# Mixer decays from running sums, an attention stage written out on TensorE, and the output bias as a one-row product

## The chip, the core and the metric

The kernel runs on one core of one Trainium2 chip. The metric is the device time of a whole execution in microseconds. The time of the kernel before is the median of three runs; one further execution was taken by the profiler, and all rows shown come from it. TensorE is written PE in the rows, VectorE DVE, ScalarE ACT, GpSimd POOL, the sync engine with its DMA queue SP.

## What is computed

A decoder layer over 32 sequences of 128 tokens with 128 features, each of its three parts followed by a layer norm. The mixer is a recurrence over tokens with four heads:

```python
alpha = jnp.exp(A_t * dt_t); beta = (1 - tr_t) * dt_t * alpha; gamma = tr_t * dt_t
base = bt * (px * beta + xt * gamma)
sr = sr * alpha + concatenate([base[..., :R] * cos(th), base[..., R:]])
si = si * alpha + base[..., :R] * sin(th)
y = sum((sr[..., :R] * cos(th) + si * sin(th)) * ct[..., :R]) + sum(sr[..., R:] * ct[..., R:])
...
x1 = layernorm(x + (y + D * x_h) * silu(z_h) @ w_out.T)
x2 = layernorm(x1 + softmax(mask(q k^T / sqrt(8))) v @ Wo + bo)
out = layernorm(x2 + shared_expert(x2) + routed_experts(x2))
```

For a pair of tokens s <= t of a sequence the factor of the recurrence is exp(sum of A*dt over the tokens after s up to t), 0 for s > t. Attention is over 16 heads of 8 features, keys and values from a context, with a mask over the keys. The bias `bo` is an input like the others. The experts are 16 with 4 chosen, out of the best 2 of 4 groups.

## The kernel before

The sequences go in groups of four (GS = 4, 512 tokens), eight groups. Three stages follow one another, each a block at whose end all engines meet: mixer, attention, experts. Each engine has its own program, written by hand; what orders the work is the position in each program and the semaphores (`sem.at(g, k)` is the k-th event of group g). `pairs` and `ahead` run the groups: `pairs` has six groups in a loop of two and the last two written out, `ahead` has four in a loop of two and the last four written out, so in attention each engine has one jump back, after group 1.

**Setup** (a block of its own) computes the small projections, dt, A and the gates on VectorE and ScalarE for two halves of the sequences, and with GpSimd the coefficients (`coefficients`, `betas`): A*dt as `decay` and in two parts `dec_hl`, `gamma` and `beta`.

**Mixer.** For each sequence b of a group, TensorE's `front(g, par, b)` (L856 to L862) makes the sums for all pairs of tokens: two products of the triangle `after` with `ramp` (L859; A*dt spread over columns by the triangle `upto`, made by GpSimd in `ramps`, L732, two operations of 512 columns a sequence), and one that adds -30000 above the diagonal (L860, bfloat16), into the bank PD. ScalarE takes the exponential of the bank in one operation of 512 columns (L693), VectorE multiplies the scores with it (`mix`, L806). `tokens` (L868) are the projections of the present and the shifted tokens, three products of 256 columns each, the first three in `front`, the others at the head of `scores`. VectorE weighs them with gamma and beta (L791, L792) and adds them (`w_tok`, L795); `back` (L900) is the product with `mix`. `scores` also has three products of `plain` (L877) and four instructions of c_rot with b_rot (L880).

A group's order on TensorE is: `theta` of the next group (L405), `skip` (L893), then for b = 1, 2, 3: `front(b)`, `back(b-1)`, `scores(b)`, and after the first two of them `features` 0, 1 and 2, 3 of the next group (L420), then features 4, 5, `front` of the next group's first sequence, `back(3)`, first scores of the next group, `mixer_output` (L285). Features 2 and 3 write the banks from which VectorE reads b_rot and c_rot, and wait for these (`freed`). The angles of a group go theta (TensorE), `angles` (ScalarE), `fractions` (VectorE, L387 and L391, two of each), `sines` (ScalarE, L368, behind an ACT_TABLE_LOAD), `rotate` (VectorE: two b_rot at L766, four c_rot at L769 and L770). VectorE's order is mix(0), fractions, inputs and mix(1), rotate, inputs and mix(2), plain_lo, inputs and mix(3), then y (L829), gates, inputs of the next group, the residual (L124) with its statistics, and the split of x (L395) that stands at the head of the next group. GpSimd's order is ramps of this group's sequences 2 and 3, ramps of the next group's 0 and 1, `steps_of`, then `normalise_pool`. In the last group it makes the third parts of k and q (`part_third`, L237) instead, and SP's queue stores and stacks these (L265, L266, L276).

**Attention.** Scores are made twice, once for the row maxima (VectorE, L1237) and once transposed for the exponential (ScalarE, L1145); masks enter by products (L1383), the scores proper are L1393. `weigh` has the products with v (L1437) and with ones (L1433). The maxima are split in three bfloat16 parts by four short VectorE operations (`split_maxima`, L1255 to L1261, tile `npart`), transposed (L1457), stored and read back by DMA (`max_scratch`, `q_stack`). `output(g)` (L1464) multiplies the normed context with `w_o`, 128 columns of float32 for each of four sequences. GpSimd's `biased` (L1081, tile `xb`) adds `b_o` to x1 ahead of it, and VectorE's residual sum (L124) reads xb and the bank. SP stages x1 by DMA for TensorE's transposes (`xs`, L1029 and `x1T`).

**Experts** isn't touched. The line by which the features wait for what frees their banks:

```python
freed = [(s_ang, 0), (s_ang, 1), (s_prod, 1), (s_prod, 3), (s_prod, 4), (s_prod, 5)]
```

Of the kernel before, what the change touches and what calls it, by code (L numbers as in the profile page):

```python
# [23 lines left out]
P = 128  # L24
NSEQ = 32
# [264 lines left out]
def mixer(nc, t, d, psum, a):  # L290

    with ExitStack() as ctx:
# [15 lines left out]
        after = sb("after", [P, P], F32R)  # L308
        acausal = sb("acausal", [P, P], BF16)
# [5 lines left out]
        gamma = sb("gamma", [P, NSEQ, HEADS])  # L315
        beta = sb("beta", [P, NSEQ, HEADS])
        decay = sb("decay", [P, NSEQ, HEADS])
        alpha = sb("alpha", [P, NSEQ, HEADS])
        dec_hl = sb("dec_hl", [P, 2, NSEQ, HEADS])
        dec_r = sb("dec_r", [P, NSEQ, HEADS], F32R)  # L320
# [6 lines left out]

        xhl = sb("xhl", [P, 2, 2, GS, P + 1], F32R)
# [5 lines left out]
        s_coef, s_alpha = (ctx.enter_context(nc.semaphore(n)) for n in ("coefficients_pool", "alpha_ready"))  # L334
# [5 lines left out]
        s_ramp = sem("ramp_ready", 8)  # L340
        s_dec = sem("decay_mm", GS)
        s_xx = sem("x_mm", GS)
        s_g = sem("g_mm", GS)
        s_exp = sem("expo_ready", GS)
        s_w = sem("w_ready", 3 * GS)
# [8 lines left out]
        P0, P1, PX, PD, PG, PY0, PY1, PO = psum  # L354
# [28 lines left out]
        def fractions(dve, g):  # L383

            for k in range(2):
                dve.wait_ge(s_ang.sem, s_ang.at(g, k))
                dve.tensor_scalar(whole[:, k, :], ang[:, k, :], ROUND, -ROUND, ALU.add, ALU.add).then_inc(s_whole.sem, 1)  # L387
            for k in range(2):
                dve.wait_ge(s_whole.sem, s_whole.at(g, k))
                dve.wait_ge(s_trig.sem, s_trig.at(g - 1, k))  # L390
                dve.tensor_tensor(frac[:, k, :], ang[:, k, :], whole[:, k, :], ALU.subtract).then_inc(s_frac.sem, 1)  # L391
# [30 lines left out]

        def coefficients(pool, half):

            seqs, n = HALVES[half], 7 * half
            dt, dec, hi, lo = soft[:, seqs, 0:4], decay[:, seqs, :], dec_hl[:, 0, seqs, :], dec_hl[:, 1, seqs, :]
            pool.tensor_tensor(dec, dec, dt, ALU.mult).then_inc(s_coef, 1)
            pool.wait_ge(s_coef, n + 1)
            pool.tensor_copy(dec_r[:, seqs, :], dec).then_inc(s_coef, 1)
            pool.tensor_tensor(gamma[:, seqs, :], gate[:, seqs, :], dt, ALU.mult).then_inc(s_coef, 1)  # L430
# [17 lines left out]
        with ExitStack() as c1:  # L448
# [40 lines left out]
            def _(pool):  # L489
                for s in (s_ramp, s_turns):  # L490
                    s.prime(pool)
# [232 lines left out]
        def _(pool):  # L724
# [1293 lines left out]
```

## Time and profile before

| what | us |
|---|---|
| median of three runs | 678.86 (673.94 to 679.98) |
| the profiled execution | 679.41 |
| its span, first to last instruction | 677.7 |
| TensorE busy in the span | 600.6 (89%), mean granted clock 0.96 of 2.4 GHz |
| VectorE, ScalarE, GpSimd busy | 498.2 (74%), 255.8 (38%), 261.2 (39%) |
| setup until the first `theta` of the groups | 0 to 45.9 |
| mixer until the last group's `skip` | 45.9 to 222.3 |
| the last group and the passage to attention | 222.3 to 251.1 |
| attention, its head and its groups | 251.1 to 473.4 |
| experts | 473.4 to 677.7 |

A row of the timeline gives the start, the time until the last of its merged instructions ends, the engine, the line of kernel.py, the operation, out<-in, the count, and in brackets how long the engine was idle before it and what ended that. Products are pipelined: a row's time is longer than the distance to the next start, and it is the distances that add up. A float32 product of the rows counts as two instructions. "issue" is idle time for which the profile shows no event waited for.

### The profile page before, as it was taken

How to read it: one execution, taken by the hardware profiler on the slowest of the kernel's cores; microseconds unless marked ns; L12 is line 12 of the kernel's file. 1: busy time of each engine (PE TensorE's matmuls, PEld its weight loads, DVE VectorE, ACT ScalarE, POOL GpSimd, SP SyncE). 2: the span in 40 equal slices, each digit the busy share in tenths (PEclk: the TensorE clock that was granted, in tenths of full speed). 3: DMA queues.
4: the chain of work that ended last, by engine and by line, in shares of the span. 5: the costliest groups of instructions: out<-in, count | busy, mean ns of one | idle time of the engine just before them, and what ended most of it. 6: DMA issues, size and time to landing. Idle time of an engine off the chain costs nothing. (4 is left out here: it accounts for less than half of the span.)

```text
span 677.7 us, 17999 instructions
## 1 busy us (share of the span) xinstructions
PE 600.6 (89%) x6368; PEld 494.8 (73%) x6368; DVE 498.2 (74%) x1246; ACT 255.8 (38%) x444; POOL 261.2 (39%) x301
## 2 busy tenths in 40 slices
PE   6589999999999855699799999877999999999994
PEld 6467777777787643578678777655888888888884
DVE  3867977977977738368688888656688787887863
ACT  2443533533543320356446655343332232232220
POOL 4264646647645628624244346091110110110111
PEclk9979999999999978699899999899999999999998
DMA  7020000000000067064464555400000000000000
GB/s 211 0 63 1 17 15 0 15 15 0 15 16 1 12 176 219 17 171 138 124 176 117 142 133 154 119 7 2 32 1 32 31 0 32 31 29 2 17 16 16
DMA packets 39186, 39.29 MB, mean 58 GB/s; under 512 B 4609, under 2 KB 30753, under 8 KB 39121
## 3 DMA queue, kind: packets, MB, share of 16 engines
q1 hardware_dynamic: 37200, 35.69, 18.4%
q0 software_dynamic: 704, 1.92, 1.1%
q10 hardware_dynamic: 1216, 0.79, 0.5%
q8 instruction: 44, 0.72, 0.5%
q14 instruction: 22, 0.17, 0.1%
HBM read 24.10 MB, written 10.88 MB: 52 GB/s over the span
## 5 line engine op out<-in xcount | busy, mean ns | idle before, releaser
L1911 PE MATMUL bank<-xT_hl_c,w_up 128*128 128x512 f32 x432 | 119.7, 413 | 2.4 <-ACTq L67 2.4
L141 POOL TENSOR_TENSOR rstd<-mv,norm_c 128x4 f32<-128x4 f32 x24 | 6.4, 268 | 272.0 <-DVE mv L135 257.1
L1237 DVE TENSOR_REDUCE nmax<-bank 128x4 f32<-128x512 f32 x112 | 72.0, 685 | 31.0 <-PE bank L1393 26.7
L1145 ACT ACTIVATE prob<-bank 128x512 f32<-128x512 f32 x128 | 69.4, 594 | 56.1 <-PE bank L1393 46.8
L1911 PEld LDWEIGHTS bank<-xT_hl_c,w_up 128*128 128x128 f32 x432 | 77.2, 192 | 16.2 <-ACTq L67 2.6
L1833 ACT ACTIVATE sg<-bank 128x512 f32<-128x512 f32 x72 | 43.0, 597 | 106.7 <-PE bank L1911 106.7
L1927 PEld LDWEIGHTS bank<-w_down,hid 128*128 128x128 f32 x576 | 74.4, 191 | 5.9 <-issue 0.5
L732 POOL TENSOR_TENSOR ramp<-upto,dec_hl 128x512 fp32r<-128x512 f32 x64 | 66.8, 1072 | 27.2 <-PE bank L860 27.2
L1927 PE MATMUL bank<-w_down,hid 128*128 128x128 f32 x576 | 75.6, 275 | 0.0
L1383 PE MATMUL bank<-neg_i,mask 64*128 64x256 bf16 x512 | 52.7, 286 | 17.9 <-ACT prob L1145 5.8
L1866 DVE TENSOR_TENSOR gu<-sg,bank 128x512 f32<-128x512 f32 x64 | 43.9, 685 | 21.9 <-PE bank L1911 10.0
L1870 DVE TENSOR_TENSOR hid<-gu,bank 128x512 f32<-128x512 f32 x64 | 44.0, 688 | 7.1 <-DVE gu L1866 1.0
L868 PE MATMUL bank<-w_x,xhl 128*128 128x256 f32 x192 | 42.2, 329 | 0.0
L1383 PEld LDWEIGHTS bank<-neg_i,mask 64*128 64x128 bf16 x512 | 16.9, 97 | 33.2 <-issue 11.7
L1437 PE MATMUL bank<-prob,v_d 128*32 128x128 f32 x1024 | 36.4, 286 | 0.0
L1433 PE MATMUL bank<-prob,ones_s 128*32 128x128 f32 x1024 | 34.6, 276 | 0.8 <-ACT prob L1145 0.8
L420 PE MATMUL bank<-xhl,w_feat 128*128 128x512 f32 (+1 forms) x96 | 29.9, 447 | 5.4 <-DVE b_rot L766 4.4
L868 PEld LDWEIGHTS bank<-w_x,xhl 128*128 128x128 f32 x192 | 29.6, 191 | 6.1 <-issue 5.3
L880 PE MATMUL bank<-c_rot,b_rot 128*128 128x256 f32 x128 | 32.8, 378 | 0.0
L1433 PEld LDWEIGHTS bank<-prob,ones_s 128*32 128x32 f32 x1024 | 26.0, 109 | 6.1 <-issue 2.2
L1437 PEld LDWEIGHTS bank<-prob,v_d 128*32 128x32 f32 x1024 | 28.2, 114 | 2.9 <-ACT prob L1145 0.2
L1071 POOL CAST mask<-mask 128x512 bf16<-128x512 uint8 x32 | 19.3, 612 | 27.3 <-PE bank L1393 22.2
(227 smaller groups left out, 1250.1 us busy)
## 6 DMA issues: line engine op xcount, KB each, us to landing
k_stack<-k_scratch SPq DMA_DIRECT2D x32, 128.0 KB, 2.7
q_stack<-q_scratch SPq DMA_DIRECT2D x32, 128.0 KB, 2.9
k_scratch<-k_part SPq DMA_DIRECT2D x16, 192.0 KB, 2.5
q_scratch<-q_part SPq DMA_DIRECT2D x16, 192.0 KB, 2.5
x<-xT_in SPq DMA_DIRECT2D x8, 256.0 KB, 8.4
mask<-mask_in SPq DMA_DIRECT2D x8, 256.0 KB, 4.7
xres<-x_in SPq DMA_DIRECT2D x8, 256.0 KB, 2.9
k_stack<-k_scratch SPq DMA_DIRECT2D x32, 64.0 KB, 3.0
```

Source lines behind the costliest of these rows:

```text
L732: pool.tensor_tensor(ramp[:, b % 2, v, :, :], bc(upto[:, None, :], [P, HEADS, P]), bc(dec_hl[:, v, bass.ds(g * GS + b, 1), :].rearrange("p ...
L868: mm = pe.matmul(PX[:, shift * D_INNER:(shift + 1) * D_INNER], xhl[:, par, a, b, 1 - shift:P + 1 - shift], w_x[:, v, :], start=(n == 0), s ...
L1145: act.activation(prob[:, b % 2, ORDER[n], :, :], (TT0, TT1)[n % 2][:, :], ACT.Exp, scale=XD ** -0.5)\
L1237: dve.tensor_reduce(nmax[:, b, 4 * u:4 * u + 4], (SS0, SS1)[n % 2][:, :].rearrange("p (i k) -> p i k", i=4), AX_X, ALU.max, negate=True).t ...
L1383: pe.matmul(banks[j][:, :].rearrange("p (i h k) -> p i h k", i=4, h=2)[:, :, half, :], mask[rows, par, b, kind + ver, :], bc(neg_i[rows, N ...
L1433: mm = pe.matmul(U1[32 * u:32 * u + 32, 0:P], ones_s[:, 4 * b + i, :, :].rearrange("p r c -> p (r c)"), prob[:, b % 2, u, i, :], start=(b ...
L1437: mm = pe.matmul(U0[32 * u:32 * u + 32, b * P:(b + 1) * P], v_d[:, par, b, i * P + 32 * u:i * P + 32 * u + 32], prob[:, b % 2, u, i, :], s ...
L1833: act.activation(sg[:, k, :], GG[k][:, :], ACT.Silu).then_inc(a_s.sem, 1)
L1866: dve.tensor_tensor(dst, sg[:, k, :], UU[k][:, :], ALU.mult).then_inc(v_gu.sem, 1)
L1870: dve.tensor_tensor(hid[:, c, :], gu[:, k, :], WW[(c - 1) % 2][:, :], ALU.mult).then_inc(v_hid.sem, 1)
L1911: mm = pe.matmul(bank[:, :], w_up[:, which, a, c, :], xT_hl[par][:, v, :], start=(n == 0), stop=(n == 2))
L1927: mm = pe.matmul(PO[:, b * P:(b + 1) * P], hid[:, c, b * P:(b + 1) * P], w_down[:, c, :], start=(c == 0 and b == 0), stop=(c == NC - 1), s ...
```

## The change

1. **Decay sums.** `ramps` and the three products of `front` go. Setup makes running sums of A*dt over the tokens (`sums`, two small products a half), copies them (`sums_out`), stores one copy in DRAM (`store_sums`), and SP's queue reads it back a row of 512 values per sequence, spread over all 128 partitions (`load_row`, 256 KB). GpSimd sets the part above the diagonal to -30000 in place (`causal`, one select of 512 columns), and ScalarE takes exp(sum(t) - sum(s)) with the second copy, `upto_s`, as bias: four operations of 128 columns a sequence (`expos`), issued one sequence ahead. `rows` has four buffers, one for each b; a row of the next group is loaded once this group's exponential has read its buffer.
2. **Tokens.** The six products of `tokens` stand together ahead of `back`, in the banks PX0 and PX1 in turn (PD's bank became free).
3. **VectorE.** The two `whole`, `frac`, `b_rot` operations are one each of double width, the four `c_rot` two, and the two `xg` one.
4. **Attention.** TensorE's groups are written out (`for g in range(NG)`), the other engines keep their loop. `x1T` reads x1 itself; `xs` and its DMA go. `biased` goes; `output` has a product of one row (`one_row` with `b_o[0:1, :]`) ahead of each product with `w_o`, and the residual reads x1.

```diff
+        def sums(pe, half, bank):
+
+            dec = decay[:, HALVES[half], :].rearrange("p b h -> p (b h)")
+            pe.wait_ge(s_coef, half + 1)
+            pe.matmul(bank[64 * half:64 * half + 64, 0:P], dec, upto[:, :], start=True, stop=True)
+            pe.matmul(bank[:, P:P + 64], upto[:, :], dec, start=True, stop=True).then_inc(s_sums, 1)
+
+        def sums_out(act, half, bank):
+
+            rows_of = slice(64 * half, 64 * half + 64)
+            act.wait_ge(s_sums, half + 1)
+            act.activation(sum_rows[rows_of, :], bank[rows_of, 0:P], ACT.Copy).then_inc(s_summed, 1)
+            act.activation(upto_s[:, HALVES[half], :].rearrange("p b h -> p (b h)"), bank[:, P:P + 64], ACT.Copy, scale=-1.0)\
+                .then_inc(s_summed, 1)
+
+        def store_sums(sp, half):
+
+            rows_of = slice(64 * half, 64 * half + 64)
+            sp.wait_ge(s_summed, 2 * half + 1)
+            sp.dma_start(rows_dram[rows_of, :], sum_rows[rows_of, :]).then_inc(s_stored, 16)
+
+        def load_row(sp, g, b):
+
+            sp.wait_ge(s_exp.sem, s_exp.at(g - 1, HEADS * b + HEADS - 1))
+            sp.dma_start(rows[:, b, :, :], rows_dram[bass.ds((g * GS + b) * HEADS, HEADS), :]
+                         .rearrange("h t -> (h t)").partition_broadcast(P).rearrange("p (h t) -> p h t", h=HEADS))\
+                .then_inc(s_row[b].sem, 16)
+
+        def causal(pool, g, b):
+
+            pool.wait_ge(s_row[b].sem, s_row[b].at(g))
+            pool.sem_inc(pool_passed, 1)
+            pool.affine_select(out=rows[:, b, :, :], in_=rows[:, b, :, :], compare_op=ALU.is_ge, fill=NEG, base=0,
+                               pattern=[[0, HEADS], [1, P]], channel_multiplier=-1).then_inc(s_sel.sem, 1)
+
+        def expos(act, g, b):
+
+            act.wait_ge(s_sel.sem, s_sel.at(g, b))
+            act.wait_ge(s_mix.sem, s_mix.at(g, b - 2))
+            for h in range(HEADS):
+                act.activation(expo[:, b % 2, h, :], rows[:, b, h, :], ACT.Exp,
+                               bias=upto_s[:, bass.ds(g * GS + b, 1), h]).then_inc(s_exp.sem, 1)
 
...
@@ fractions
-            for k in range(2):
-                dve.wait_ge(s_ang.sem, s_ang.at(g, k))
-                dve.tensor_scalar(whole[:, k, :], ang[:, k, :], ROUND, -ROUND, ALU.add, ALU.add).then_inc(s_whole.sem, 1)
...
+            dve.wait_ge(s_ang.sem, s_ang.at(g, 1))
+            dve.tensor_scalar(whole[:, :, :], ang[:, :, :], ROUND, -ROUND, ALU.add, ALU.add).then_inc(s_whole.sem, 2)
+            dve.wait_ge(s_whole.sem, s_whole.at(g, 1))
+            dve.wait_ge(s_trig.sem, s_trig.at(g - 1, 1))
+            dve.tensor_tensor(frac[:, :, :], ang[:, :, :], whole[:, :, :], ALU.subtract).then_inc(s_frac.sem, 2)
...
@@ rotate
+                dve.wait_ge(s_trig.sem, s_trig.at(g, 1))
+                dve.tensor_tensor(b_rot[:, par, :, :], bc(P0[:, None, :], [P, 2, GT]), trig[:, :, :], ALU.mult).then_inc(s_prod.sem, 2)
...
@@ scalar group
                 for b in range(GS):
-                    act.wait_ge(s_dec.sem, s_dec.at(g, b))
-                    act.wait_ge(s_mix.sem, s_mix.at(g, b - 2))
-                    act.activation(expo[:, b % 2, :, :], PD[:, :], ACT.Exp).then_inc(s_exp.sem, 1)
+                    if b < GS - 1:
+                        expos(act, g, b + 1)
+                    elif left:
+                        expos(act, g + 1, 0)
...
@@ gpsimd group
-                ramps(g, (2, 3))
-                if left:
-                    ramps(g + 1, (0, 1))
                 if left == 2:
                     steps_of(pool, g + 2)
                 if left:
+                    for b in range(GS):
+                        causal(pool, g + 1, b)
                     normalise_pool(pool, g, s_res, s_x1, res, mv, rstd, norm_c, x1[:, bass.ds(g * GS, GS), :])
...
@@ attention, output
                 for b in range(GS):
-                    mm = pe.matmul(U1[:, b * P:(b + 1) * P], ctxT[:, b, :], w_o[:, :], start=True, stop=True)
+                    pe.matmul(U1[:, b * P:(b + 1) * P], one_row[:, :], b_o[0:1, :], start=True, stop=False)
+                    mm = pe.matmul(U1[:, b * P:(b + 1) * P], ctxT[:, b, :], w_o[:, :], start=False, stop=True)
...
-            ahead(pe, group)
+            for g in range(NG):
+                group(g, g % 2, NG - 1 - g)
```

How the order changes on TensorE in the mixer's loop, from the products for b = 2 to the 96-column features; before:

```order
L859 MATMUL bank<-ramp,after 128x512 x2
L860 MATMUL bank<-acausal,ident 128x512
L862 REGISTER_ALU
L868 MATMUL bank<-w_x,xhl 128x256 x3
L898 REGISTER_ALU
L900 MATMUL bank<-mix,w_tok 64x128 x4
L868 MATMUL bank<-w_x,xhl 128x256 x3
L877 MATMUL bank<-plain 128x512 x3
L880 MATMUL bank<-c_rot,b_rot 128x256 x2
L416 ISA
L420 MATMUL bank<-xhl,w_feat 96x512 x3
```

and now:

```order
L907 REGISTER_ALU
L910 MATMUL bank<-w_x,xhl 128x256 x6
L938 REGISTER_ALU
L939 REGISTER_ALU
L941 MATMUL bank<-mix,w_tok 64x128 x4
L918 MATMUL bank<-plain 128x512 x3
L921 MATMUL bank<-c_rot,b_rot 128x256 x2
L418 ISA
L422 MATMUL bank<-xhl,w_feat 96x512 x3
```

The ramp and mask products are gone, the second three token products moved from behind `back` to ahead of it; the 96-column features still come behind the c_rot products.

VectorE in the mixer's loop, from mix(1) over `rotate` to the inputs of b = 2; before:

```order
L806 TENSOR_TENSOR mix<-bank,expo 128x512
L763 ISA
L766 TENSOR_TENSOR b_rot<-bank,trig 128x512 x2
L767 REGISTER_ALU
L769 TENSOR_TENSOR c_rot<-bank,trig 64x512
L770 TENSOR_TENSOR c_rot<-bank,trig 64x512
L769 TENSOR_TENSOR c_rot<-bank,trig 64x512
L770 TENSOR_TENSOR c_rot<-bank,trig 64x512
L790 REGISTER_ALU
L791 ISA
L791 TENSOR_TENSOR xg<-bank,gamma 128x256
L792 REGISTER_ALU
```

and now:

```order
L856 TENSOR_TENSOR mix<-bank,expo 128x512
L813 ISA
L815 TENSOR_TENSOR b_rot<-bank,trig 128x1024
L816 REGISTER_ALU
L819 TENSOR_TENSOR c_rot<-bank,trig 64x2x512 x2
L838 REGISTER_ALU
L839 ISA
L839 TENSOR_TENSOR xg<-bank,shares 128x512
L843 REGISTER_ALU
L845 TENSOR_TENSOR w_tok<-xg 128x256
```

Nothing changed places; b_rot and c_rot are one and two operations of double width, and the inputs one of 512 columns.

TensorE in attention, at the end of group 1, with the output products and the jump back; before:

```order
L1383 MATMUL bank<-neg_i,mask 128x4x64 x4
L1393 MATMUL bank<-k_stack,q_stack 128x128 x8
L1464 MATMUL bank<-w_o,ctxT 128x128 x4
L103 REGISTER_ALU
L103 COMPARE_AND_BRANCH
L1383 MATMUL bank<-neg_i,mask 128x4x64 x4
L1393 MATMUL bank<-q_stack,k_stack 128x128 x8
L1383 MATMUL bank<-neg_i,mask 128x4x64 x4
```

and now, at the same place:

```order
L1409 MATMUL bank<-neg_i,mask 128x4x64 x4
L1419 MATMUL bank<-k_stack,q_stack 128x128 x8
L1490 MATMUL bank<-b_o,one_row 128x128
L1491 MATMUL bank<-w_o,ctxT 128x128
L1490 MATMUL bank<-b_o,one_row 128x128
L1491 MATMUL bank<-w_o,ctxT 128x128
L1490 MATMUL bank<-b_o,one_row 128x128
L1491 MATMUL bank<-w_o,ctxT 128x128
L1490 MATMUL bank<-b_o,one_row 128x128
L1491 MATMUL bank<-w_o,ctxT 128x128
L1409 MATMUL bank<-neg_i,mask 128x4x64 x4
L1419 MATMUL bank<-q_stack,k_stack 128x128 x8
```

The jump is gone, and each output product has one of the bias ahead of it.

## Rows read from the trace of the kernel before

**Rows 1.** windows, mixer and attention: us, busy (x) per engine, clock, DMA

```profile
45.90:222.30 176.40, 171.19 (x1064) 136.18 (x1063) 142.10 (x286) 72.16 (x105) 94.51 (x91) 1.00 0.03 9
...
285.90:440.00 154.10, 141.69 (x3123) 114.77 (x3123) 120.98 (x260) 81.24 (x155) 59.57 (x73) 0.98 0.51 141
```

**Rows 2.** timeline, mixer group 3: start, us, engine, line, x, [idle <-releaser]

```profile
116.89 0.66 PE L900 MATMUL bank<-mix,w_tok 128*64 128x128 f32 x8
...
124.48 0.63 PE L859 MATMUL bank<-ramp,after 128*128 128x512 f32 x2
...
125.62 0.66 PE L900 MATMUL bank<-mix,w_tok 128*64 128x128 f32 x8
...
126.21 0.62 PE L868 MATMUL bank<-w_x,xhl 128*128 128x256 f32 x3
...
126.67 0.86 PE L877 MATMUL bank<-plain 96*128 96x512 f32 x3
...
130.56 0.73 PE L859 MATMUL bank<-ramp,after 128*128 128x512 f32 x2 [0.76 <-POOL ramp L732]
...
142.14 0.66 PE L900 MATMUL bank<-mix,w_tok 128*64 128x128 f32 x8
```

**Rows 3.** timeline of the same group, the chain to c_rot's readers

```profile
124.36 0.68 DVE L806 TENSOR_TENSOR mix<-bank,expo 128x512 f32<-128x512 f32 x1
...
126.04 1.28 DVE L391 TENSOR_TENSOR frac<-ang,whole 128x512 f32<-128x512 f32 x2
...
126.81 1.28 ACT L368 ACT_TABLE_LOAD   x1 [0.76 <-DVE frac L391]
...
128.11 1.16 ACT L368 ACTIVATE trig<-frac 128x512 f32<-128x512 f32 x2
...
129.13 1.29 DVE L766 TENSOR_TENSOR b_rot<-bank,trig 128x512 f32<-128x512 f32 x2
...
134.22 1.77 PE L420 MATMUL bank<-xhl,w_feat 128*96 128x512 f32 x6
```

**Rows 4.** lines in the mixer's window: busy us, mean ns, idle before

```profile
L900 PE MATMUL bank<-mix,w_tok 128*64 128x128 f32 x224 | 18.4, 285 | 1.0 <-DVE mix L806 1.0
```

**Rows 5.** timeline of setup, a ScalarE operation of 128 columns

```profile
23.73 0.31 ACT L554 ACTIVATE e<-e 128x128 f32<-128x128 f32 x1
```

**Rows 6.** page, DMA issues: xcount, KB each, us to landing

```profile
xres<-x_in SPq DMA_DIRECT2D x8, 256.0 KB, 2.9
```

**Rows 7.** timeline, the mixer's last group: GpSimd, TensorE, SP's queue

```profile
230.39 4.04 POOL L732 TENSOR_TENSOR ramp<-upto,dec_hl 128x512 fp32r<-128x512 f32 x4
...
232.48 0.72 PE L859 MATMUL bank<-ramp,after 128*128 128x512 f32 x2 [2.92 <-POOL ramp L732]
...
244.50 4.02 SPq L276 DMA_DIRECT2D q_stack<-q_scratch  x8
```

**Rows 8.** timeline, TensorE in attention, behind the jump and later

```profile
332.34 0.39 PE L1383 MATMUL bank<-neg_i,mask 64*128 64x256 bf16 x4 [2.49 <-issue]
...
337.79 1.08 PE L1433 MATMUL bank<-prob,ones_s 128*32 128x128 f32 x32
...
357.58 0.39 PE L1383 MATMUL bank<-neg_i,mask 64*128 64x256 bf16 x4
...
361.46 1.08 PE L1433 MATMUL bank<-prob,ones_s 128*32 128x128 f32 x32
```

**Rows 9.** timeline of attention: output product, xb, npart, a DMA wait

```profile
356.49 1.16 PE L1464 MATMUL bank<-w_o,ctxT 128*128 128x128 f32 x8
...
371.74 1.30 POOL L1081 TENSOR_TENSOR xb<-x,b_o 128x512 f32<-128x512 f32 x1
...
371.85 1.24 DVE L1257 TENSOR_TENSOR nrest<-nmax,npart 128x32 f32<-128x32 f32 x1
...
375.11 0.27 PE L1457 MATMUL bank<-ident,npart 128*48 128x128 bf16 x2 [1.10 <-DVE npart L1261]
...
432.70 0.61 PE L1383 MATMUL bank<-neg_i,mask 64*128 64x256 bf16 x4 [2.90 <-DMA q_stack<-max_scratch]
```

More of the change, by code:

```diff
@@ L485, in _ @@
                 sp.dma_start(a.cin[:, :, :], d["ctxT"][:, 0:2 * GT].rearrange("p (g t) -> p g t", t=GT)).then_inc(s_att, 16)
+                for b in range(GS):
+                    s_row[b].prime(sp)
+                store_sums(sp, 0)
+                sp.wait_ge(s_stored, 16)
+                for b in range(GS):
+                    load_row(sp, 0, b)
+                store_sums(sp, 1)
                 sp.wait_ge(s_att, 9 * 16)
@@ L489, in _ @@
             def _(pool):
-                for s in (s_ramp, s_turns):
+                for s in (s_sel, s_turns):
                     s.prime(pool)
@@ L533, in _ @@
                 pe.wait_ge(s_pool, 2)
+                sums(pe, 0, PX0)
                 theta(pe, 0)
@@ L536, in _ @@
                 features(pe, 0, 0, (0, 1))
+                sums(pe, 1, PX1)
             @block.scalar
@@ L655, in group @@
                     .then_inc(s_x.sem[par], 16)
+                if left:
+                    for b in range(GS):
+                        load_row(sp, g + 1, b)
                 if not left:
@@ L742, in group @@
                 if left:
+                    for b in range(GS):
+                        causal(pool, g + 1, b)
                     normalise_pool(pool, g, s_res, s_x1, res, mv, rstd, norm_c, x1[:, bass.ds(g * GS, GS), :])
@@ L747, in group @@
                 if left == 1:
-                    pool.memset(a.first[1][:, :, :, :].bitcast(F32), TWO_ONES).then_inc(a.ones, 1)
+                    pool.memset(a.first[1][:, :, :].bitcast(F32), TWO_ONES).then_inc(a.ones, 1)
+            for b in range(2):
+                causal(pool, 0, b)
             coefficients(pool, 1)
-            ramps(0, (0, 1))
             betas(pool, 1)
             steps_of(pool, 1)
+            for b in range(2, GS):
+                causal(pool, 0, b)
             pairs(pool, group)
@@ L915, in group @@
                 for b in range(1, GS):
-                    front(g, par, b)
+                    tokens(g, par, b)
                     back(g, b - 1)
@@ L931, in group @@
                 if left:
-                    front(g + 1, 1 - par, 0)
+                    tokens(g + 1, 1 - par, 0)
                 back(g, GS - 1)
@@ L941, in _ @@
             features(pe, 0, 0, range(2, 6))
-            front(0, 0, 0)
+            tokens(0, 0, 0)
             first_scores(0, 0)
@@ L1021, in _ @@
         def _(sp):
-            for s in (d_xs, d_xs):
-                s.prime(sp)
             def loads(g, par):
```

163 lines of the change are left out of this document (66 added, 97 removed).

## Prediction

> **What bounds the kernel now.** I read the stages first, then TensorE's idle lines in order of time, then what the other engines do around them. By the windows view [rows 1] TensorE is busy 171.2 of 176.4 us while the mixer's groups run at the full granted clock, and 141.7 of 154.1 us in attention. VectorE has 142.1 and 121.0. So TensorE is the bound of both stages, VectorE is next, and an operation taken off TensorE is worth its own time only until VectorE's chain is reached. The experts' stage isn't touched.
>
> In one mixer group [rows 2] the reader is to see what the decay product costs: from the first L859 to the first L900 1.14 us, of which the three L868 products take 0.46 (the same three from 126.21 to 126.67), so the two ramp products and the mask product take 0.68 us. They stand four times in a group. One more front waited 0.76 us for GpSimd's ramp. From back(3) of a group to back(0) of the next it is 8.73 us, from back(0) to back(3) 16.52.
>
> Beside it runs a chain that TensorE so far just covers [rows 3]: mix(0) ends at 125.04, the two fractions at 127.32, then the table load, the two sines (129.27), b_rot and four c_rot operations, and features 2 and 3 (L420 from 134.22).
>
> **The mixer's groups.** Removed from TensorE: four fronts, 4 x 0.68 = 2.7 us, and the ramp wait, 0.76. If nothing else held, a group would be 3.4 us shorter. I walk the chain instead. The fractions become one operation, so the table load, which waits for the fractions, can start only after the whole pair: mix(0) end + 2.2, table 1.28, sines 1.16, hand-overs 0.15, so sines end at +4.8 (before: 129.27 - 125.04 = +4.2). b_rot, one operation instead of two, I price at 1.22 (two took 1.29), and each c_rot of double width the same: +8.5 us. Feature product 3 waits for both c_rot, so it starts at +8.6; before it started half way through 134.22 + 1.77, at +10.1. Behind it: 0.9 for itself, six token products 0.9; VectorE meanwhile does xg, w_tok and mix(2), about 1.9 after c_rot, so back(2) is at +10.5. Then 0.6 (back), 1.2 (scores), 1.7 (gate features) and 0.9 (tokens): back(3) at +15.0 to 15.1. I take 15.1 against 16.52: 1.4 us less from back(0) to back(3), though TensorE's own work there fell by 3 x 0.68 + 0.76 = 2.8. So feature product 3 will wait about 1.4 us for c_rot, a wait that isn't there now.
> From back(3) to the next back(0) TensorE loses one front, 0.68: 8.05. VectorE's chain y, gates, inputs, residual, statistics, split and mix(0) took 125.04 - 116.89 = 8.15 from the same start and loses 0.07 where two xg operations become one. So 8.1, a gain of 0.6. In two of the seven boundaries TensorE waits about 0.5 for mix(0) already, 1.0 in all [rows 4]; there VectorE's chain is the bound and I count 0.1.
> Over the groups: 5 x 0.6 + 2 x 0.1 = 3.2, and 6 x 1.4 plus 0.6 for the first group (which has no ramp wait) = 9.0. Together -12.2 us.
>
> What this adds is hidden. ScalarE's exponential becomes four operations of 128 columns; the one of that size in the trace took 0.31 us [rows 5], so 1.24 a sequence, four sequences 5 us of a group of 24. They run a sequence ahead; only the sines are behind them, and these wait longer for the fractions. Each row load is 256 KB; a load of that size landed 2.9 us after its issue [rows 6], and each is issued a whole group ahead, so some 18 us of delay would still be covered. Its cost is 0, at most the 3 us once. GpSimd's causal select is as wide as a ramp operation (about 1 us, [rows 7]) with one where two stood.
>
> **Setup.** The sums go through DRAM before the mixer's groups; this lies beside VectorE's softplus work. The second copy of the sums stands behind the sines, so the barrier comes about 1.2 us later (0.5 for the merged fractions, 0.6 for two short copies [rows 5]); the first front, at the low clock, is gone: -0.9. I count +0.3; bounds 0 and +4 (a store and a load of 2.9 us each, less what covers them).
>
> **The mixer's end** [rows 7]. The last group's ramps hold GpSimd 4.04 us from 230.39; only then comes the third part of k (L237), for which SP's queue waits before it issues stores and stacks nearly back to back, the last until 248.52. Behind it stands the barrier to attention. Without ramps the whole SP chain moves up by 4.0. TensorE's wait of 2.92 for a ramp falls in the same time and isn't counted again. -4.0 us, bounds -2 and -6.
>
> **Attention.** Written out, TensorE has no jump back. At the jump it was idle 2.49 us for "issue", and the stretch to the next L1433 took 337.79 - 332.34 = 5.45 us, where the same stretch a group later took 361.46 - 357.58 = 3.88 [rows 8]. So 2.49 + 1.57, -4.0 us; 0 if straight code of that length has to be fetched as slowly.
> The bias: per group four products of one row in float32 are added to four that took 357.58 - 356.49 = 1.09 us [rows 9]. A one-row product isn't in the trace. From below: the 128x32 products of rows 8, 32 in 1.08 us, 0.03 each, 8 per group, 0.3; from above the full 1.09 x 2 for a badly overlapped weight load. I take 1.09, the row of the same width and type: 8 x 1.09 = 8.7. Once it is hidden, at 432.70, where TensorE waits 2.90 us for the maxima's DMA: 7.6 remain.
> GpSimd's sum: xb took 1.30 us, and VectorE's tiny L1257 beside it 1.24 us; it ended 0.05 us after xb. TensorE then waited 1.10 us for npart (375.11) [rows 9]; such waits of about 1 us come before four of the max_rows. With xb gone at most 1.1 a group is won, at least 0. I take 0.6: five groups, -3.0.
> The Trainium skill (SBUF — State Buffer, SBUF: two separate sides) says that VectorE and GpSimd share a port pair as an exclusive lock held for a whole instruction. The trace agrees (1.24 us beside 1.30). By this rule GpSimd's next operation takes xb's place and VectorE may wait as long for that: the term would be near 0 and the sum 667.1.
> The staging load of x1 and its wait go; no wait on it is seen, so 0. Attention: -4.0 + 7.6 - 3.0 = +0.6.
>
> **The sum.** The profiled execution took 679.4 us (span 677.7), 0.5 above the median of 678.86. +0.3 - 12.2 - 4.0 + 0.6 = -15.3: 664.1 us. I say 664.
>
> **Rivals.**
> Full gain on TensorE: the chain to c_rot proves looser (trig starts before the fractions end, or VectorE runs ahead). Then the groups give 7 x 2.8, less 0.8 in the first, which has no ramp wait, and 7 x 0.7 at the boundaries: 23.7 instead of 12.2, so 664.1 - 11.5 = 652.6. For it: VectorE idles 34 us of the stage. Against: the walked chain.
> VectorE holds the mixer's pace: selects beside VectorE's short operations and the later sines take the gain back. Then only the ramp waits go, 5 x 0.8 = 4.0, and the end: 679.4 + 0.3 - 4.0 - 4.0 + 0.6 = 672.3. For it: VectorE's 142 us; against: it has fewer operations.
> Dear bias product: each costs twice the row, 8.7 more: 673.
> Slower: the new waits of 1.4 us per group, with the smaller ones at the boundaries, let the granted clock fall to its lower level of 1.2 GHz. After the jump, 2.49 us idle was followed by 1.57 us of lost time; 14 gaps of that kind cost 22 us, 664 + 22 = 686. It decides from some 10 such gaps. Against: the granted clock was 1.00 over the whole stage [rows 1], with waits of 0.76 in it, and up to 2.92 just behind it.
>
> **Chances.** Forecast 0.50, full gain 0.18, VectorE's pace 0.18, dear bias 0.07, clock 0.07. A measurement tells about 1% (6.8 us) from no change. Below 672.1 lie the first two, and somewhat over half of the third: faster 0.79; its rest, the dear bias and a tail of the first: same 0.15; slower 0.06. The range takes the full gain with the bounds of end and setup below it (650), and VectorE's pace with part of the bounds of bias and setup above it (676).
>
> **What would show it.** Right: L900's first to last in a group 15.1 us instead of 16.5; a wait of the second three of L420's 96-column products on c_rot of 1 to 1.5 us; no wait for a ramp; SP's last stack of the mixer ends near 232.6 (248.52 + 0.3 - 12.2 - 4.0); L1490 and L1491 together 2.2 us; no "issue" gap near the third group of attention. Wrong: features 3 without a wait (then 653), a granted clock below 1.00 in the mixer, or an exponential that TensorE or VectorE waits for.

## The result, and the profile after

The kernel after took 674.5 us in the median of its runs, the kernel before 678.1 in the same comparison: 0.9944 of before, with a 95% interval from 0.9922 to 0.9966. By the medians it is 3.6 us faster (3.8 by the ratio), a gain clear of the noise but a quarter of the 15 us forecast, and within the 1% that the prediction called no change. The time lies inside the predicted range.

The profiled execution shows where the rest went. The first lines of its page:

```profile
span 674.4 us, 18009 instructions
## 1 busy us (share of the span) xinstructions
PE 609.4 (90%) x6344; PEld 502.4 (74%) x6344; DVE 481.6 (71%) x1174; ACT 277.5 (41%) x544; POOL 205.5 (30%) x253
```

TensorE has fewer products than before (6344 against 6368) and is busy 8.8 us longer (609.4 against 600.6). By the stages of the windows view it is busy 26.3 us longer in attention (214.0 against 187.7). Something there became dearer by more than the mixer's decay products were worth.

**The mixer.** The same marks as in [rows 2, 3], one group of after (start, us, engine, line, what, times, idle before and releaser):

```profile
119.90 0.66 PE L941 MATMUL bank<-mix,w_tok 128*64 128x128 f32 x8
...
128.47 0.94 PE L422 MATMUL bank<-xhl,w_feat 128*96 128x512 f32 x3 [1.01 <-DVE c_rot L819]
...
134.71 0.66 PE L941 MATMUL bank<-mix,w_tok 128*64 128x128 f32 x8
```

```profile
119.12 0.69 DVE L856 TENSOR_TENSOR mix<-bank,expo 128x512 f32<-128x512 f32 x1
...
120.90 1.23 DVE L393 TENSOR_TENSOR frac<-ang,whole 128x1024 f32<-128x1024 f32 x1
...
124.81 1.23 DVE L815 TENSOR_TENSOR b_rot<-bank,trig 128x1024 f32<-128x1024 f32 x1 [0.90 <-ACT trig L372]
125.95 2.47 DVE L819 TENSOR_TENSOR c_rot<-bank,trig 64x1024 f32<-64x1024 f32 x2
```

From back(0) to back(3) it is 14.81 us, from mix(0)'s end to feature product 3 8.66. The skip of the last group starts at 207.47 (before 222.33), 14.9 us earlier. At the mixer's end:

```profile
225.89 3.83 SPq L276 DMA_DIRECT2D q_stack<-q_scratch  x8
```

```profile
232.30 3.70 PE L285 MATMUL bank<-w_out,y 128*128 128x128 f32 x16 [6.73 <-issue]
```

The last stack ends at 229.72 (248.52 in [rows 7]), and attention's first product stands at 232.30, where before it stood at 251.10. The mixer thus gave 18.8 us.

**Attention** gave it back. The experts' first product starts at 468.93 (before 473.39): 236.6 us after attention's first in place of 222.3, so 14.3 longer. The experts' stage itself, though not touched, took 205.5 us in place of 204.3. With these three figures (-18.8, +14.3, +1.2) the two spans agree. One group's output product, which answers to the first row of [rows 9]:

```profile
317.50 0.39 PE L1419 MATMUL bank<-k_stack,q_stack 48*128 48x128 bf16 x8
317.81 0.48 PE L1490 MATMUL bank<-b_o,one_row 1*128 1x128 f32 x2
318.23 0.30 PEld L1491 LDWEIGHTS bank<-w_o,ctxT 128*128 128x128 f32 x2
318.23 0.49 PE L1491 MATMUL bank<-w_o,ctxT 128*128 128x128 f32 x2
318.65 0.48 PE L1490 MATMUL bank<-b_o,one_row 1*128 1x128 f32 x2
...
320.72 0.49 PE L1491 MATMUL bank<-w_o,ctxT 128*128 128x128 f32 x2
321.14 0.61 PE L1409 MATMUL bank<-neg_i,mask 64*128 64x256 bf16 x4
```

From 317.81 to 321.14 it is 3.33 us, where the four w_o products alone took 1.09. The one-row products do not only add their own time: a w_o product, 0.27 us before as the mean of four, now takes 0.42 as well. PEld is the load of the stationary tile: here it starts together with its own product, not beside the one before. The windows around it (length, busy time of each engine, TensorE's granted clock, share and rate of the DMAs) show a second loss behind it:

```profile
318.00:320.00 2.00, 2.00 (x11) 1.40 (x11) 1.85 (x4) 0.73 (x2) 0.26 (x1) 1.00 0.60 200
320.00:322.00 2.00, 2.00 (x20) 1.51 (x22) 0.00 (x0) 0.00 (x0) 0.00 (x0) 0.79 0.02 7
322.00:324.00 2.00, 2.00 (x36) 1.61 (x36) 0.93 (x2) 1.60 (x3) 0.03 (x1) 0.50 0.03 8
```

TensorE's row shows no gap, and yet the granted clock falls from 1.00 to 0.50, its level of 1.2 GHz. From the first L1490 to the next query projection it is 7.91 us here (317.81 to 325.72), and 6.33 in a group whose clock stays up (344.08 to 350.41), so the fall costs 1.6 us. It happens behind the products of five of the eight groups, four times for 3.4 us. Behind the last group the clock stays low from 464.5 to 474.7, across the passage to the experts, where it is low in the kernel before too, but for 3.4 us (from 473.5).

### The profile page after: what moved, and what is told of

Its sections match the earlier page's. It is cut to its first block and busy times, and to the rows that moved or that the text cites. A ratio compares the mean times of both kernels' runs of the same rounds, so it can differ in the third digit from the quotient of the medians.

```text
span 674.4 us, 18009 instructions
## 1 busy us (share of the span) xinstructions
PE 609.4 (90%) x6344; PEld 502.4 (74%) x6344; DVE 481.6 (71%) x1174; ACT 277.5 (41%) x544; POOL 205.5 (30%) x253
## 5 line engine op out<-in xcount | busy, mean ns | idle before, releaser
L1409 PE MATMUL bank<-neg_i,mask 64*128 64x256 bf16 x512 | 54.3, 293 | 12.0 <-ACT prob L1173 5.4
L477 ACT ACTIVATE expo<-rows,neg_sums 128x128 f32<-128x128 f32 x128 | 40.8, 390 | 13.3 <-DVE mix L856 13.2
L422 PE MATMUL bank<-xhl,w_feat 128*128 128x512 f32 (+1 forms) x96 | 32.1, 459 | 10.2 <-DVE c_rot L819 5.6
L921 PE MATMUL bank<-c_rot,b_rot 128*128 128x256 f32 x128 | 32.9, 378 | 0.0
L469 POOL TENSOR_SCALAR_AFFINE_SELECT rows<-rows 128x512 f32<-128x512 f32 x32 | 20.8, 670 | 39.1 <-DMA rows<-sum_rows_scratch 33.9
L422 PEld LDWEIGHTS bank<-xhl,w_feat 128*128 128x128 f32 (+1 forms) x96 | 17.3, 190 | 18.3 <-DVE c_rot L819 9.6
L918 PE MATMUL bank<-plain 96*128 96x512 f32 x96 | 30.7, 428 | 0.0
L910 PEld LDWEIGHTS bank<-w_x,xhl 128*128 128x128 f32 x192 | 27.9, 193 | 3.3
```

The lines of the kernel that those rows point to most:

```text
L422: mm = pe.matmul(bank[0:m, :], w[:, i, :], xhl[:, par, v, :, 1:], start=(n == 0), stop=(n == 2))
L477: act.activation(expo[:, b % 2, h, :], rows[:, b, h, :], ACT.Exp, bias=upto_s[:, bass.ds(g * GS + b, 1), h]).then_inc(s_exp.sem, 1)
L1409: pe.matmul(banks[j][:, :].rearrange("p (i h k) -> p i h k", i=4, h=2)[:, :, half, :], mask[rows, par, b, kind + ver, :], bc(neg_i[rows, N ...
```

## The experiments

"Ratio" is against the runs of the kernel before that were taken together with it; their medians lie between 677.8 and 680.6 us, so small gaps are better read from the ratios. All times are medians, that of rows_64 of two runs only.

| kernel | us | ratio (95%) |
|---|---|---|
| attention_alone | 690.6 | 1.0181 (1.0164 to 1.0199) |
| after | 674.5 | 0.9944 (0.9922 to 0.9966) |
| rows_32 | 672.2 | 0.9916 (0.9877 to 0.9955) |
| rows_64 | 667.8 | 0.9853 (0.9788 to 0.9918) |
| mixer_alone | 666.3 | 0.9801 (0.9737 to 0.9866) |
| wide_bias | 659.7 | 0.9718 (0.9661 to 0.9776) |
| bias_first | 659.4 | 0.9709 (0.9675 to 0.9743) |
| full_rows | 657.3 | 0.9704 (0.9681 to 0.9727) |
| staged2 | 655.3 | 0.9635 (0.9590 to 0.9680) |
| xb_again | 654.9 | 0.9639 (0.9603 to 0.9676) |
| xb_back | 654.2 | 0.9615 (0.9564 to 0.9665) |
| no_bias | 653.5 | 0.9605 (0.9554 to 0.9657) |
| frac_split | 650.9 | 0.9582 (0.9538 to 0.9626) |

**mixer_alone and attention_alone** take one half of the change each: the function `attention` of one kernel is put into the other.

> The mixer's change alone: attention is that of the kernel before. Theory A (the mixer keeps its whole gain and attention's own edits lose it): in the two traces attention's first product starts 18.8 us earlier (251.10 to 232.30), so 678.1 - 18.8 = 659 us, give or take 2 for the granted clock at attention's start. Rival B (whatever comes behind the shorter mixer gives the time back, by the lower clock in attention's head or by DMAs that now collide): from attention's first product to the experts' 236 us as after, not 222, and a time of 670 or more.

> Attention's change alone, behind the mixer of the kernel before. If the two halves add, it is after less mixer_alone, 674.5 - 666.3 = +8, on 679: 687 us, slower than before, with the one-row products at 3.3 us a group. If the loss needs the new mixer (its earlier end meets attention's DMAs or a lower clock), it is near 679 or below.

The mixer alone gives 2.0%, attention alone costs 1.8%. They add within their intervals: 0.9801 x 1.0181 = 0.998, after is 0.994 (attention_alone is 3.6 us above the 687 expected). So the mixer's gain was not lost by being early: attention's own edits lose it, behind either mixer. mixer_alone is 7 us above what theory A wanted, though. Its attention starts 20.1 us earlier (230.98) but takes 229.0 us instead of 222.3, and 3 us of these stand in the group with the jump back:

```profile
310.98 1.16 PE L1505 MATMUL bank<-w_o,ctxT 128*128 128x128 f32 x8
316.00 0.61 PE L1424 MATMUL bank<-neg_i,mask 64*128 64x256 bf16 x4 [3.86 <-issue]
```

The same gap took 2.49 us in [rows 8]; here it is 3.86, and the clock is low behind it until near 322.

**no_bias and xb_back** both drop the one-row product; xb_back puts GpSimd's sum back.

```diff
-pe.matmul(U1[:, b*P:(b+1)*P], one_row[:, :], b_o[0:1, :], start=True, stop=False)
-mm = pe.matmul(U1[:, b*P:(b+1)*P], ctxT[:, b, :], w_o[:, :], start=False, stop=True)
+mm = pe.matmul(U1[:, b*P:(b+1)*P], ctxT[:, b, :], w_o[:, :], start=True, stop=True)
```

and in xb_back also:

```diff
+pool.tensor_tensor(xb[:, :, :], x1[:, bass.ds(g * GS, GS), :], bc(b_o[:, None, :], [P, GS, P]), ALU.add).then_inc(g_x.sem, 1)
...
-residual_sum(dve, g - 1, U1, x1[:, bass.ds((g - 1) * GS, GS), :], g_out, v_res, res)
+dve.wait_ge(g_x.sem, g_x.at(g - 1))
+residual_sum(dve, g - 1, U1, xb[:, :, :], g_out, v_res, res)
```

> The kernel after with the bias b_o left out: neither the one-row product nor GpSimd's sum is done, so this is the bound of what any form of it can give. Theory A (the product costs 2.25 us a group of its own, and the clock falls behind it in five of eight groups, 1.55 us each): -18 - 8 = -26, of which VectorE's chain to npart takes back up to 4: 648 to 652 us, and the granted clock is 1.00 where L1491 ends. Rival B (only the one-row products' own time counts and the falls of the clock have other causes): -18 + 4, 660, with falls near the same places. Rival C (the product is hidden, the head of attention holds the pace): over 668.

> The kernel after with GpSimd's sum of x1 and the bias back in place of the one-row product; the rest of attention stays written out. Theory A: as no_bias, plus the waits for npart that the sum brings back (11.2 us in before against 6.6 in after): 652 to 657 us. By the forecast's own terms the product would cost 7.6 and the sum 3.0, so this kernel would be only 4.6 faster than after: 670. The lock rule of the Trainium skill (SBUF - State Buffer, section SBUF: two separate sides) would have GpSimd's sum cost nothing beyond what takes its place: then it equals no_bias.

no_bias leaves the bias out of the result. Theory A holds for both in the main, though no_bias stands 1.5 us above its range: without the product 21.0 us less than after, with GpSimd's sum in its place 20.3 less. In neither does the clock fall between 272 and 420 us, where after has four falls, three of them behind output products and one behind a gap (285.67, below). What GpSimd's sum costs is seen in the waits of TensorE for the maxima's parts (xb_back):

```profile
307.49 0.27 PE L1495 MATMUL bank<-ident,npart 128*48 128x128 bf16 x2 [1.01 <-DVE npart L1299]
...
331.04 0.27 PE L1495 MATMUL bank<-ident,npart 128*48 128x128 bf16 x2 [1.05 <-DVE npart L1299]
```

The same waits take 0.33 and 0 us in no_bias. Over a group that is 0.7 us (xb_back 297.95 to 307.49, 9.54 from one L1495 row to the next, against 8.85 in no_bias), 2.3 us by the profiled spans, 0.8 by the medians.

**Why is the product dear?** wide_bias and bias_first keep one row and take away the turns; full_rows keeps the turns and takes away the one row.

In wide_bias:

```diff
-for b in range(GS):
-    pe.matmul(U1[:, b * P:(b + 1) * P], one_row[:, :], b_o[0:1, :], start=True, stop=False)
+pe.matmul(U1[:, :].rearrange("p (b d) -> p b d", b=GS), one_row[:, :], bc(b_o[0:1, None, :], [1, GS, P]), start=True, stop=False)
+for b in range(GS):
```

In bias_first:

```diff
     pe.matmul(U1[:, b * P:(b + 1) * P], one_row[:, :], b_o[0:1, :], start=True, stop=False)
+for b in range(GS):
     mm = pe.matmul(U1[:, b * P:(b + 1) * P], ctxT[:, b, :], w_o[:, :], start=False, stop=True)
```

In full_rows:

```diff
-one_row = sb("one_row", [1, P])
+one_row = sb("one_row", [P, P])
-pool.memset(one_row[:, :], 1.0).then_inc(g_one, 1)
+pool.memset(one_row[:, :], 1.0 / P).then_inc(g_one, 1)
-pe.matmul(U1[:, b * P:(b + 1) * P], one_row[:, :], b_o[0:1, :], start=True, stop=False)
+pe.matmul(U1[:, b * P:(b + 1) * P], one_row[:, :], b_o[:, :], start=True, stop=False)
```

> The kernel after with one one-row product over 512 columns (the bias repeated four times) in place of four over 128, ahead of the four products by w_o. Theory A1 (the cost lies in the change between a one-row and a 128-row weight tile, which stands eight times in the mixed form and twice here): the four w_o products take 1.1 us again and the bias some 0.9, 2.0 in place of 3.33, and the clock stays up: -11 - 8, 656 us; with the falls staying 664. Rival A2 (a one-row product in float32 is dear for each column, 0.42 us for 128): 1.66 + 1.1 = 2.8, -4: 670. Rival A3 (float32 products into a bank that holds a sum are slow, first or second): no change, 674.

> The kernel after with its four one-row products of 128 columns ahead of the four products by w_o, not in turns with them. Theory A1 (what is dear is the change between a one-row and a 128-row tile): the one-row products take 1.1 us as the w_o products did alone, 2.2 us a group in place of 3.33, and the granted clock stays at its full value behind them: 674.5 - 9 - 8 = 658 to 662 us. Rival A4 (a one-row product of 128 columns takes 0.42 us wherever it stands, and a w_o product only behind one): 1.66 + 1.1 = 2.8 us, 665 to 670. Rival A3 (any float32 product that adds to a sum of another tile is slow): 674.

> The kernel after with the bias product over all 128 rows (each stationary element 1/128, the moving tile the bias on every partition), in turns with the products by w_o as in after: the same count, columns and order, only the rows differ. Theory A1: 0.27 us a product, 2.2 us a group, and no fall of the clock behind it: 658 to 662 us. Rival A5 (turns of any two weight tiles are slow, or it is the number of products): 3.33 us a group stays, 674. Should the falls of the clock come from rows that stand idle, they go here; should they stay though a product takes 0.27 us, they come from something else.

bias_first leaves part of the computation out: the Trainium skill (PSUM — Partial Sum Buffer, The four PSUM rules) says that a product which starts a sum clears the written marks of its whole bank; by this rule only the last one's bias of four one-row products in a row reaches the output. The number of instructions is unchanged.

A1 holds in all three on the product and on the clock; in time wide_bias stands 3.7 us above its 656 and full_rows 0.7 below its range. wide_bias:

```profile
312.21 1.12 PE L1489 MATMUL bank<-b_o,one_row 1*128 1x512 f32 x2
313.26 1.16 PE L1492 MATMUL bank<-w_o,ctxT 128*128 128x128 f32 x8
```

bias_first:

```profile
314.21 1.15 PE L1490 MATMUL bank<-b_o,one_row 1*128 1x128 f32 x8
315.30 1.16 PE L1492 MATMUL bank<-w_o,ctxT 128*128 128x128 f32 x8
316.39 0.39 PE L1409 MATMUL bank<-neg_i,mask 64*128 64x256 bf16 x4
```

full_rows:

```profile
311.99 0.49 PE L1490 MATMUL bank<-b_o,one_row 128*128 128x128 f32 x2
312.21 0.30 PEld L1491 LDWEIGHTS bank<-w_o,ctxT 128*128 128x128 f32 x2
312.32 0.39 PE L1491 MATMUL bank<-w_o,ctxT 128*128 128x128 f32 x2
...
312.76 0.39 PE L1491 MATMUL bank<-w_o,ctxT 128*128 128x128 f32 x2
312.99 0.39 PE L1490 MATMUL bank<-b_o,one_row 128*128 128x128 f32 x2
313.21 0.39 PE L1491 MATMUL bank<-w_o,ctxT 128*128 128x128 f32 x2
...
313.98 0.39 PE L1409 MATMUL bank<-neg_i,mask 64*128 64x256 bf16 x4
```

The one-row products side by side take 1.09 us for four, just the price that the forecast gave them, and the w_o products keep theirs. In turns over 128 rows a product starts every 0.22 us, and the load of the next tile (L1491 at 312.21) starts 0.11 us ahead of its product. Only the turns of a one-row tile with a 128-row tile cost 0.42 us a product.

One price explains all of these rows: 0.22 us a product, and 0.20 us for each change between such tiles, the last one to the 64-row mask product included. That gives 4 x 0.22 + 0.20 = 1.09 for w_o alone, 8 x 0.22 + 0.20 = 1.98 for full_rows (1.99 measured, 311.99 to 313.98), 2.18 with two changes for bias_first (2.18, 314.21 to 316.39), and 3.38 with eight for after (3.33). So the 0.27 us of a product in a block of four is the 0.22 with its share of one change.

And in all three the granted clock stays at 1.00 where it fell in after: the window 316.00 to 318.00 of bias_first, just behind the eight products, reads

```profile
316.00:318.00 2.00, 2.00 (x53) 1.73 (x55) 0.77 (x2) 0.89 (x2) 0.00 (x0) 1.00 0.04 8
```

bias_first is 2 us above full_rows although it was to be equal. Its one change more a group is worth 8 x 0.20 = 1.6 us of that; its trace, of an execution of 663.3 us, also has six "issue" gaps of 5.8 us in all between 260 and 445 us, full_rows one of 0.8.

**rows_64 and rows_32** are full_rows with fewer rows; for 64:

```diff
-one_row = sb("one_row", [P, P])
+one_row = sb("one_row", [64, P])
-pool.memset(one_row[:, :], 1.0 / P).then_inc(g_one, 1)
+pool.memset(one_row[:, :], 1.0 / 64).then_inc(g_one, 1)
-pe.matmul(U1[:, b * P:(b + 1) * P], one_row[:, :], b_o[:, :], start=True, stop=False)
+pe.matmul(U1[:, b * P:(b + 1) * P], one_row[:, :], b_o[0:64, :], start=True, stop=False)
```

> As full_rows, but the bias product spans 64 rows (each stationary element 1/64): does any tile with fewer rows than its neighbour cost the turns their overlap, or only one of a single row? Theory A6 (every change between tiles of different rows): 0.83 us for a pair, 3.33 us a group, falls of the clock behind it, 672 to 676 us. Rival A7 (few rows are the trouble): 0.45 to 0.6 us for a pair, 1.8 to 2.4 us a group, no fall: 656 to 661 us.

> As rows_64 with 32 rows (1/32 each). Theory A6: 0.83 us for a pair and 672 to 676 us, as with 1 and with 64 rows. Rival A7: between the two, pairs of 0.5 to 0.83 us, dearer than with 64 rows.

In rows_64:

```profile
312.30 0.39 PE L1419 MATMUL bank<-k_stack,q_stack 48*128 48x128 bf16 x8
312.47 0.30 PEld L1490 LDWEIGHTS bank<-b_o,one_row 64*128 64x128 f32 x2
312.52 0.44 PE L1490 MATMUL bank<-b_o,one_row 64*128 64x128 f32 x2
...
313.31 0.48 PE L1490 MATMUL bank<-b_o,one_row 64*128 64x128 f32 x2
313.72 0.49 PE L1491 MATMUL bank<-w_o,ctxT 128*128 128x128 f32 x2
314.14 0.48 PE L1490 MATMUL bank<-b_o,one_row 64*128 64x128 f32 x2
```

A6 is right on the product: 0.83 us a pair with 64 rows, 0.83 with 32 (338.82 to 339.65), 0.83 with one. So it is not the fewness of the rows but the change between 128 and 64 or fewer. Not every difference costs, though, and here A6 goes too far. The 64-row bias product follows scores of 48 rows with no loss: it starts 0.22 us behind their row (312.30 to 312.52), its load ahead of it, where after's one-row product needs 0.31 (317.50 to 317.81) and its load isn't ahead. The mask products of 64 rows and the scores of 51 and 48 stand in turns in every kernel with their loads ahead (in rows_64 scores of 51 rows load from 311.74 and start at 311.85, the next mask products from 312.02 and 312.07). In the mixer of after the 128-row L921 follows the 96-row L918 with its load at 125.50, ahead of the product at 125.73.

A6 was wrong on the clock as well: with 64 rows no fall is seen between 267 and 457 us, with 32 rows there are four ahead of the passage, with one row five behind the products. rows_64's time met neither range. It gives the turns' own price without the clock: 14 us over no_bias (17 by the ratios), where 8 x 2.24 = 18 us of product were added and some waits (the maxima's parts, a DMA) were filled by them. The remaining 6 to 7 us of after are about what its falls cost, an estimate from the 1.6 us of one.

**staged2** parts the jump from the staging of x1: it is xb_back with x1 staged by a DMA. A first form, staged, kept the unused `one_row`; its staging tile needs 4096 bytes a partition where 4000 are left, so it has no time. staged2 leaves `one_row` out.

```diff
+sp.wait_ge(p_x.sem, p_x.at(g - 2))
+sp.dma_start(xs[:, par, :, :], x1[:, bass.ds(g * GS, GS), :]).then_inc(d_xs.sem[par], 16)
-transpose_x1(pe, a, t, x1[:, g * GS:(g + 1) * GS, :], PO)
+transpose_x1(pe, a, t, xs[:, par], PO)
```

> As xb_back (attention written out, GpSimd's sum), but x1 staged by a DMA into a tile of its own before it is transposed, as in before: it parts the staging from the jump. xb_back stands 12 us below mixer_alone, whose attention is that of before. Theory J (the jump back and the lowered clock behind it are the whole): no change, 654 us. Rival S (the staging loads hold the queue behind them, seen as waits for q_stack of 0.96 and 0.70 us in mixer_alone and none in xb_back): 656 to 658, with these waits back.

> xb_back once more, word for word, in five rounds, as the foot of the two others of this call and for the interval of the best version so far: 654 us, 0.9615 of before.

Theory J: 655.3 against 654.9, and the waits for q_stack's load from q_scratch (0.96 and 0.70 us in mixer_alone) are not back, so the staging is worth nothing. staged2 and mixer_alone now differ by TensorE's loop alone, 0.9635 against 0.9801: written-out code is worth some 11 us by the medians, 7.6 by the profiled spans (655.0 and 662.6). At the place of the jump, staged2 has no gap:

```profile
310.91 1.16 PE L1507 MATMUL bank<-w_o,ctxT 128*128 128x128 f32 x8
312.00 0.39 PE L1426 MATMUL bank<-neg_i,mask 64*128 64x256 bf16 x4
```

**frac_split** tests the chain to c_rot.

```diff
-dve.tensor_scalar(whole[:, :, :], ang[:, :, :], ROUND, -ROUND, ALU.add, ALU.add).then_inc(s_whole.sem, 2)
+for k in range(2):
+    dve.tensor_scalar(whole[:, k, :], ang[:, k, :], ROUND, -ROUND, ALU.add, ALU.add).then_inc(s_whole.sem, 1)
...
-dve.tensor_tensor(frac[:, :, :], ang[:, :, :], whole[:, :, :], ALU.subtract).then_inc(s_frac.sem, 2)
+for k in range(2):
+    dve.tensor_tensor(frac[:, k, :], ang[:, k, :], whole[:, k, :], ALU.subtract).then_inc(s_frac.sem, 1)
```

> xb_back with the fractions of the mixer computed in two halves again, as in before; b_rot and c_rot stay merged. It tests the step of the forecast by which c_rot's chain sets back(2): the table load starts when the first half is there, some 0.5 us sooner, VectorE's wait for the sines (0.90 us at 124.81) nearly goes, and with it the wait of feature product 3 for c_rot (0.62 to 1.01 us, six times, 5.6 us in all per the line of groups). If the chain is what binds: 3 us less, 651. If VectorE's own count of instructions binds (two more of them a group, 0.1 to 0.2 us each): no change or 1 us more, 655.

The chain binds: 4 us less than xb_again beside it. The intervals of the two overlap, but attention's first product also stands 4.5 us earlier (226.93 against 231.44) and the experts' 4.6 (444.41 against 449.01). Feature products in xb_again, setup's included, by the line of groups (busy us, mean ns, idle before and its releasers):

```profile
L422 PE MATMUL bank<-xhl,w_feat 128*128 128x512 f32 (+1 forms) x96 | 31.4, 448 | 10.9 <-DVE c_rot L819 5.6 <-DVE b_rot L815 5.2
```

and in frac_split:

```profile
L424 PE MATMUL bank<-xhl,w_feat 128*128 128x512 f32 (+1 forms) x96 | 31.8, 459 | 6.3 <-DVE b_rot L817 3.8 <-DVE c_rot L821 2.5
```

4.6 us less idle time before one line. Joining the fractions, a part of the change that reads like a saving (1.23 us for one operation against 1.28 for two), held the table load back and cost the change about that much. frac_split is the best version found: 0.9582 of before, 24 us under after.

## Why the prediction was right and wrong

**Mixer's groups: right, a little short.** Forecast -12.2 with +0.3 for setup, so -11.9; the last group's skip is 14.9 us earlier. The walked chain was exact: feature product 3 was to start 8.6 us behind mix(0)'s end, and started 8.66 behind. It waited for c_rot as foretold, but 0.62 to 1.01 us instead of 1.4, and back(0) to back(3) is 14.5 to 14.8 in the first six groups instead of 15.1; the seventh has 13.80 and no such wait. Inside the groups this gave 12.4 us up to the last one, where 9.0 were forecast. The boundaries gave 2.2 where 3.2 were forecast: five of 8.1 to 8.2 as foretold, two of 9.34, no shorter than before (9.31 and 9.32), where TensorE waits 1.18 us for mix(0). frac_split shows that the chain is what binds.

**Cover of the exponentials: right.** Four of them were to take 1.24 us a sequence and took 1.28:

```profile
120.02 1.28 ACT L477 ACTIVATE expo<-rows,neg_sums 128x128 f32<-128x128 f32 x4 [1.44 <-DVE mix L856]
```

In the mixer's groups neither TensorE nor VectorE waits for one.

**Mixer's end: right.** -4.0 forecast, -3.9 measured (18.8 less 14.9).

**Jump: the right kind, too small, and in after hidden.** Forecast -4.0; mixer_alone against staged2 gives -7.6 to -11. The bound at the other end, straight code that must be fetched as slowly, was partly true as well: after shows

```profile
285.67 0.39 PE L1409 MATMUL bank<-neg_i,mask 64*128 64x256 bf16 x4 [1.68 <-issue]
```

with a low clock behind it that costs 1.57 us (285.67 to the first L1490 at 291.00 takes 5.33, and 3.76 from 314.05 to 317.81). In this kernel these 3.25 us eat most of the 4.06 that the gap of [rows 8] cost; in xb_back and staged2 the first gap is 1.08 and 0.46 and the clock stays up. The Trainium skill (Runtime: NRT & Kernel Launch, Instruction fetch mechanics) says that a taken branch out of the fetched window stalls for a fetch and that straight code hides it mostly. The traces agree: 2.49 and 3.86 us at the jump, 0.73 to 1.68 for the longest gap of straight code in after, xb_back and staged2. That these gaps are fetches no row shows; they are "issue".

**The bias product: the step that failed.** Forecast 1.09 us a group, 8.7 in all, 7.6 behind the DMA wait; measured 2.24 a group, 18 in all, and five falls of the clock, of some 1.6 us each where two groups can be compared, together 20.3 us against GpSimd's sum (after against xb_back), where the forecast's terms gave 4.6. The rate was taken from four w_o products in a row. Such a rate holds for one-row products in a row too, as bias_first shows, but it says nothing of two kinds in turns: the next tile's load, which starts ahead of its product in full_rows, waits in after, 0.20 us at each change between one row and 128. The "dear bias" rival had the right price (twice the row) and got 0.07; it lacked the clock. The prediction's bound from above, 1.09 x 2 for a badly overlapped weight load, was the truth, and the sum went by the lower price.

**The clock in attention: not in the sum.** The slower rival looked for lower clocks in the mixer, behind idle gaps. The mixer's groups kept 1.00. The falls came in attention, in stretches where TensorE's row shows no idle time.

**GpSimd's sum: the right kind, a little too large.** -3.0 forecast; no_bias is under xb_back by 0.8 in the medians and 2.3 in the spans, with 0.7 us a group in the waits. The Trainium skill's lock rule (SBUF — State Buffer, SBUF: two separate sides), by which the term was to be near 0, is borne out no better than the forecast's 3.0 by these runs: the medians lie nearer to it, the waits do not.

**The sum.** Up to attention -18.8 us came where -15.9 was forecast. In attention +14.3 came where +0.6 was forecast, and TensorE's rows account for it nearly: product +17.9, jump -0.8 (4.06 gone, 3.25 new), the falls behind the products some +7, the waits for the maxima's parts -4.6 (11.2 before, 6.6 after) and those for loads of q_stack -5.0 (5.0 before, none after), +14.5 together. The waits are shorter because the longer products fill them, as the prediction had it for one of them. The 1.2 us of the experts' stage, forecast as 0, stand where the low clock of the passage lasts 10.2 us instead of 3.4.

## What to carry to other kernels

Don't put float32 products on 128 rows in turns with products on 64 or fewer: put each kind into a block, or fill the smaller one up to the rows of its neighbour. Count the changes, and look in the rows whether a tile's load starts ahead of its product. Price an added product by a row in which its neighbours are the same too, not only its shape. A bias that another engine adds at 0.1 to 0.3 us a group was cheaper here than every form of the product tried, and two operations joined into one delay whoever needed the first half.

## What the runs showed of the hardware that was not expected

- Two float32 products of 128 columns in turns start 0.42 us apart if one stands on 1, 32 or 64 rows and the other on 128, 0.22 if both have 128. A block of four with 1 or 128 rows takes 1.09 us, 0.22 each and one change of 0.20. The Trainium skill (TensorE: Matmul & The Clock Gate, Step-by-step: what each phase is for) says that the row count does not matter for a weight load, and that the next load is pulled ahead where row groups don't conflict or where it goes to the background weight buffer. The load itself agrees: 186 ns on average with one row, 191 with 128. The pulling ahead is seen between tiles of 128 rows, of 48 or 51 and 64, and at 128 behind 96. It is not seen between 128 rows and 64, 32 or 1, nor where the mixer's 64-column `mix` tile follows tiles of 128 columns (in after load and product both stand at 124.35). By what rule the two kinds part, no run here tests.
- The granted clock falls to 0.50 behind such turns while TensorE's row shows no gap: five groups of eight with one row, four with 32, none between 272 and 445 us with 64 or 128, and none there with one-row products in a block. It isn't the length of the turns alone, for those with 64 and with 32 rows take the same 0.83 us a pair. What in the turns brings the fall stays open.
- The jump back of a loop of this length cost TensorE 2.49 us in one kernel and 3.86 in another, with a low clock of 1.6 to 2.8 us' worth behind it. Straight code had gaps of up to 1.68 us.
